# The transfers of the rows of maxima move from SyncE's queue to ScalarE's queue in a two-layer decoder kernel

## The chip, the core and the metric

The kernel runs on one core of a Trainium2 chip, as one launch. The time is that of the device in microseconds (us). A core has five engines that each work through their own instructions in order: TensorE (PE in the profile, its weight loads PEld), VectorE (DVE), ScalarE (ACT), GpSimd (POOL) and SyncE (SP), which here only issues transfers. Semaphores are all that ties them together.

## What is computed

Eight batches of x (256 tokens of 128 features) pass through six residual blocks, each on a layer norm of x:

```python
x = x + _L0_attn_ref(...)    # causal linear attention, 16 heads
x = x + _L0_xattn_ref(...)   # cross attention to 512 context tokens, 16 heads, masked softmax
x = x + _L0_ffn_ref(...)     # 8 experts, the best two by gate
x = x + _L1_attn_ref(...)    # causal attention in a window of 128, 16 heads
x = x + _L1_xattn_ref(...)   # cross attention, 8 heads, then layer norms and a ReLU FFN
x = x + _L1_ffn_ref(...)     # ternary weights, GELU FFN
```

In the softmax blocks the scores are q k / sqrt(head size), the largest score of each query is taken off, then follow exp, the sum over keys, and the product with the values.

## The kernel before

**Phases.** Each batch has four attention cores, `p` = 0 (linear), 1 (cross, 16 heads), 2 (window, 16 heads) and 3 (cross, 8 heads). Between two cores of a batch runs a *chain* ("to0", "to1", "to2", "to3", "end"): it normalizes the last core's outputs, projects them, adds them to x, runs the experts or the FFN, takes a layer norm and makes the next q, k and v. Three chains run side by side, in three lanes.

**Stacks.** q and k are each split into three BF16 parts, so that six products give an f32 score. The parts are written to a DRAM buffer of the lane (`bounce`, `spread` at L591 to L596) and read back as tall stacks: 48 rows per head hold the products, and further rows hold the negated maximum of each query (`QP`, `QW`, `KS`; `chain_steps` of SyncE, L605 to L638). There are three slots for stacks.

**Maxima.** For p = 1, 2 and 3 the *max stream* computes all scores once (PE L978 to L982), DVE reduces each to its maximum (L1467 to L1475), and per group of four heads GpSimd splits the negated maxima in three parts (L795 to L799). PE then turns them into rows (L970), and DVE copies these rows from PSUM to `mrow` (L1462), a ring of four buffers. This last step is a *turn*. There are 32 turns of p = 1, 32 of p = 2 and 16 of p = 3, 80 in all. After each turn the rows are sent by transfers into the stack of queries: two for p = 1 or 2 (L656), four for p = 3 (L652), 192 in all.

**Exponentials.** The *exp stream* computes the scores a second time (PE L1004 to L1013), now with the maxima in the stack taken off, into two PSUM banks; ACT takes exp (L1199, 512 units; for p = 0 DVE masks them at L1485), and PE multiplies by the values in quads of four units (L1039). ACT copies finished outputs out (L1206). Before the first unit of a group PE waits for that group's rows (`mrow_in`).

**The order of the work** is fixed when the program is built. `plan()` simulates the three lanes and the two streams with costs written by hand and gives each event a due time; `weave` merges, for each engine, the max events, the exp events and the steps of the three lanes by due time into one sequence. Every engine uses the same events and leaves out those it has no part in. A turn's due time is that of its last maximum plus `TURN_LATE` = 3.0. So an engine that waits at one event holds up all that stands behind it in its own sequence, of whatever lane or stream. At a turn SyncE waits for the copy on DVE (`max_used`), and then for the stack itself (`stack_in`), which has then been in use by the max stream.

ACT takes part in the exp stream, and in each chain: it makes the normalized rows (L1082), copies turned activations out of PSUM for the next matmul (L1075, L1136), keeps and casts q and k (L1107 to L1130), and computes the exponentials and GELUs of the FFNs. It has no part in the max stream: `program(nothing, exp_event, chain_steps, prelude())`.

Of the kernel before, what the change touches and what calls it, by code (L numbers as in the profile page):

```python
# [16 lines left out]
B, S, D, SK = 8, 256, 128, 512  # L17
# [3 lines left out]
PARTS = 3  # L21
# [23 lines left out]
MAX_ROWS = 4 * PARTS  # L45
HALF_ROWS = NPROD * 8
# [4 lines left out]
LANES, SLOTS, WIDES, OUTS, OB, QN, MROWS = 3, 3, 2, 3, 1, 3, 4  # L51
# [226 lines left out]
TURN_N = {(e.core.p, e.core.b, e.g): i for i, e in enumerate(TURNS)}  # L278
# [5 lines left out]
IN_SLOT, OUT_BEFORE = {}, {}  # L284
# [77 lines left out]
def weave(lanes):  # L362

    at = [next(lane, None) for lane in lanes]
    while any(t is not None for t in at):
        i = min((t, i) for i, t in enumerate(at) if t is not None)[1]
        at[i] = next(lanes[i], None)


def events_of(events, act):  # L370
    for e in events:
        yield e.at
        act(e)


def runs_of(lane, steps):
    for run in RUNS:
        if run.lane == lane:
            for at in steps(run):
                yield run.at(at)  # L380


def decoder(nc, x, ctxT, maskq, maskk, weights, columns, rows_in, experts_bias, out):
    with ExitStack() as ctx:
# [6 lines left out]
        def sem(name):  # L391
            return ctx.enter_context(nc.semaphore(name))

        def sems(n, *names):
            return [[sem(f"{name}_{i}") for i in range(n)] for name in names]

        def sbs(n, name, shape, dt=F32):
            return [sb(f"{name}{i}", shape, dt) for i in range(n)]
# [24 lines left out]
        QP = sbs(SLOTS, "QP", [P, 16, S], BF16)  # L423
        QW = sbs(WIDES, "QW", [P, 8, S], BF16)
# [7 lines left out]
        mrow = sbs(MROWS, "mrow", [MAX_ROWS, S], BF16)  # L432
# [52 lines left out]
        max_scores, max_used, nm_ready = sem("max_scores"), sem("max_used"), sem("nm_ready")  # L485
# [4 lines left out]
        stack_in, = sems(SLOTS, "stack_in")  # L490
        mrow_in, = sems(MROWS, "mrow_in")
# [9 lines left out]
        def w(name, lo=0, n=None):  # L501
            a, b = W_COLS[name]
            return W[:, a + lo:(a + lo + n) if n else b]
# [19 lines left out]
        def slot_emptied(eng, run):  # L523

            old, _, _ = IN_SLOT[run.new.p, run.b]
            if old:
                eng.wait_ge(av_done, UNITS_TO[old.p, old.b])
# [20 lines left out]
        def program(max_event, exp_event, chain_steps, *more):  # L548
            weave([events_of(MAX_EVENTS, max_event), events_of(EXP_EVENTS, exp_event)]
                  + [runs_of(lane, chain_steps) for lane in range(LANES)] + list(more))  # L550
# [7 lines left out]
        def _(sp):  # L558
# [24 lines left out]
            def ctx_loads(lane):  # L583
                for run in (r for r in CTX_RUNS if r.lane == lane):
                    last = [r for r in CTX_RUNS if r.lane == run.lane and r.start < run.start]
                    yield max(run.start - 8 * STRETCH, last[-1].end if last else 0)
                    if last:
                        sp.wait_ge(lane_free[run.lane], N_RUNS(last[-1]) + 1)
                    sp.dma_start(cT[run.lane][:], ctxT[run.b:run.b + 1].rearrange("o p t -> p (o t)")).then_inc(ctx_in[run.lane], 16)
# [47 lines left out]
                if p == 3:  # L637
                    sp.dma_start(QW[core.wide][HALF_ROWS:64], back[NPROD * 16:NPROD * 16 + 16, :, 0:S]).then_inc(stack_in[slot], 16)  # L638

            def max_event(e):  # L640
                if e.kind != "turn":
                    return
                core, g = e.core, e.g
                ring = TURN_N[core.p, core.b, g] % MROWS
                row_ = mrow[ring]
                sp.wait_ge(max_used, e.n + 3)

                sp.wait_ge(stack_in[core.slot], IN_SLOT[core.p, core.b][2])
                if core.p == 3:
                    for j in range(4):  # L650
                        at = HALF_ROWS + 2 * PARTS * (j % 2)
                        sp.dma_start(QW[core.wide][at:at + PARTS, 4 * g + j, :], row_[PARTS * j:PARTS * (j + 1), :]).then_inc(mrow_in[ring], 16)  # L652
                else:
                    for r in range(2):
                        at = 64 * r + HALF_ROWS
                        sp.dma_start(QP[core.slot][at:at + MAX_ROWS, 4 * g + r:4 * g + 4:2, :],  # L656
                                     row_[:].unsqueeze(1).to_broadcast([MAX_ROWS, 2, S])).then_inc(mrow_in[ring], 16)

            program(max_event, nothing, chain_steps, *(ctx_loads(lane) for lane in range(LANES)))
            sp.wait_ge(x_out, B * 16)  # L660

        @block.gpsimd
# [404 lines left out]
        def _(act):  # L1067
# [123 lines left out]
            def exp_event(e):  # L1191
# [8 lines left out]
                elif e.kind == "keep":  # L1200
# [4 lines left out]
                        act.wait_ge(filled[last.lane], fill(last, "outputs"))  # L1205
                    nc.scalar.copy(OT[core.out][:, 2 * e.g:2 * e.g + 2, :].rearrange("p g q -> p (g q)"), ob[:, e.n % OB, :]).then_inc(out_kept, 1)  # L1206

            def prelude():
                yield 18.0
                act.wait_ge(w_in[3], 16)  # L1210
                for i in range(2):
                    ins = nc.scalar.activation(wtmp[:, i, :], w(("up", "down")[i]), ACT.Abs, accum_out=absum[:, i:i + 1])
                ins.then_inc(act_const, 1)
                yield 24
                act.wait_ge(ternary_ready, 1)

            program(nothing, exp_event, chain_steps, prelude())

        @block.vector
        def _(dve):  # L1220
# [336 lines left out]
```

## Times and profile before

| | us |
|---|---|
| median of three runs | 1142.5 |
| lowest, highest | 1141.14, 1148.11 |
| the profiled execution: its own time | 1149.97 |
| its span | 1148.3 |
| busy: PE, PEld | 867.2, 484.1 |
| busy: DVE, ACT, POOL | 664.9, 496.5, 327.2 |
| granted clock of TensorE, mean | 0.898 |

The span is that of the recorded instructions, and what lies around it is 1.67 us. Busy time does not count SyncE's issues, nor the time in which ACT or any other engine waits for a semaphore. The profile comes from one execution that is 7.5 us longer than the median.

### The profile page before, as it was taken

Reading aid. Unit: us, or ns where it says so; the run is one execution under the profiler, and the core shown is the slowest. Engines: PE = TensorE matmul, PEld = TensorE weight load, DVE = VectorE, ACT = ScalarE, POOL = GpSimd, SP = SyncE. Lnnn points to the kernel's source line nnn. Section 1 sums busy time; section 2 is a strip of 40 time slices with the busy share of each in tenths; the row PEclk is TensorE's granted clock in tenths of the full one; section 3 lists DMA queues with packets and bytes.
Section 4 is the critical chain, followed back from the end, with each engine's and each line's share of the span. In section 5 each row is a group of like instructions: output and inputs, shape, how many; then the busy total and the mean of one; then the engine's idle time right before and its main releaser. Section 6 shows DMA issues by size and latency. Waiting matters only on the chain.

```text
span 1148.3 us, 19620 instructions
## 1 busy us (share of the span) xinstructions
PE 867.2 (76%) x6459; PEld 484.1 (42%) x6522; DVE 664.9 (58%) x2234; ACT 496.5 (43%) x1019; POOL 327.2 (28%) x872
## 2 busy tenths in 40 slices
PE   0576757989887887878787677887988777875666
PEld 0354534334333443434443455653533435652345
DVE  5656546767677664766667574376566484334431
ACT  1332314544545443545464333654545334652432
POOL 7414323111212221323212235322222124341032
PEclk9888879999999988989889888999999698896877
DMA  5467764033021214541233434652120602224100
GB/s 177 113 98 160 166 147 90 19 49 53 20 48 30 38 32 85 110 97 52 56 56 68 71 80 104 143 86 39 34 53 16 103 2 52 66 64 75 16 1 10
DMA packets 124965, 79.85 MB, mean 70 GB/s; under 512 B 8312, under 2 KB 122176, under 8 KB 124736
## 3 DMA queue, kind: packets, MB, share of 16 engines
q1 hardware_dynamic: 124864, 78.59, 33.4%
q8 instruction: 52, 0.85, 0.3%
q14 instruction: 49, 0.40, 0.1%
HBM read 43.99 MB, written 32.90 MB: 67 GB/s over the span
## 4 chain that ended last, share of the span: by engine, by line
PE 46%; DVE 18%; issue 10%; DMA 9%; POOL 6%; ACT 6%; SPq 4%; another core or an unknown queue 0%; DVEq 0%; POOLq 0%; ACTq 0%
PE ob L1039 8%; PE mb L982 5%; DMA KS<-bounce 4%; PE side L858 3%; DMA QW<-bounce 3%; PE eb L1009 3%; DVE junk L1467 3%; PE eb L1010 2%; PE side L913 2%; DVE mx L1475 2%; PE side L905 2%; PE side L896 2%; DVE An L1407 2%; PE side L925 1%; PE eb L1004 1%
## 5 line engine op out<-in xcount | busy, mean ns | idle before, releaser
L1199 ACT ACTIVATE probs<-eb 128x512 f32<-128x512 f32 (+1 forms) x512 | 287.6, 570 | 379.3 <-PE eb L1010 162.1
L1467 DVE CUSTOM_DVE_ANT_0 junk<-mb,maskq_add 128x512 bf16<-128x512 f32 x256 | 172.2, 690 | 118.3 <-PE mb L982 90.0
L795 POOL TENSOR_SCALAR nm<-mx 128x8 bf16<-128x8 f32 x80 | 20.3, 254 | 455.5 <-DVE mx L1467 206.5
L1039 PE MATMUL ob<-probs,V 128*32 128x256 f32 (+1 forms) x2048 | 142.1, 399 | 1.9 <-ACT probs L1199 0.7
L1475 DVE TENSOR_REDUCE mx<-mb 128x1 f32<-128x512 f32 x128 | 84.9, 687 | 68.3 <-PE mb L982 66.5
L1009 PE MATMUL eb<-maskk_add,identb 128*128 128x512 bf16 x256 | 100.1, 391 | 6.5 <-DMA QP<-mrow 2.7
L982 PE MATMUL mb<-KS,QP 128*128 128x512 bf16 x230 | 89.3, 395 | 13.5 <-DVE mx L1467 12.8
L1010 PE MATMUL eb<-QP,KS 128*128 128x512 bf16 x233 | 91.2, 391 | 0.0
L1039 PEld LDWEIGHTS ob<-probs,V 128*32 128x32 f32 x2048 | 56.2, 115 | 79.1 <-issue 49.0
L1470 DVE CUSTOM_DVE_ANT_0 junk<-mb,winq_add 128x128 bf16<-128x128 f32 x128 | 37.1, 290 | 77.1 <-PE mb L979 75.3
L982 PE MATMUL mb<-KS,QW 112*128 112x512 bf16 x128 | 53.1, 433 | 32.7 <-DMA QW<-bounce 19.2
L818 PE MATMUL side<-ident,hn 128*128 128x128 f32 x80 | 19.6, 332 | 66.3 <-ACT hn L1082 66.2
L1206 ACT COPY OT<-ob 128x512 f32<-128x512 f32 x56 | 32.6, 582 | 68.9 <-PE ob L1033 48.0
L1485 DVE TENSOR_TENSOR probs<-eb,tri 128x512 f32<-128x512 f32 x64 | 42.1, 685 | 32.0 <-PE eb L999 30.6
L715 POOL TENSOR_TENSOR xs<-xs,scratch 128x256 f32<-128x256 f32 (+1 forms) x32 | 30.4, 951 | 104.0 <-ACT scratch L1130 63.2
L858 PEld LDWEIGHTS side<-ident,OT 128*128 128x128 f32 x448 | 55.7, 198 | 8.0 <-issue 6.7
L1013 PE MATMUL eb<-QW,KS 112*128 112x256 bf16 x256 | 51.5, 298 | 9.5 <-DMA QW<-mrow 3.1
L858 PE MATMUL side<-ident,OT 128*128 128x36 f32 (+1 forms) x448 | 55.6, 280 | 3.8 <-issue 3.7
L703 POOL TENSOR_SCALAR rstd<-mv 128x2 f32<-128x2 f32 x64 | 19.6, 307 | 134.3 <-DVE mv L1263 131.5
L982 PEld LDWEIGHTS mb<-KS,QP 128*128 128x128 bf16 x256 | 25.7, 101 | 69.9 <-DVE mx L1467 40.9
L1082 ACT ACTIVATE hn<-X,nshift,rstd 128x128 f32<-128x128 f32 x80 | 35.1, 488 | 45.8 <-POOL nshift L710 45.8
L1471 DVE CUSTOM_DVE_ANT_0 junk<-mb,winq_add 128x256 bf16<-128x256 f32 x128 | 53.7, 419 | 0.2 <-issue 0.2
(188 smaller groups left out, 1728.3 us busy)
## 6 DMA issues: line engine op xcount, KB each, us to landing
QP<-bounce SPq DMA_DIRECT2D x48, 256.0 KB, 5.6
KS<-bounce SPq DMA_DIRECT2D x32, 384.0 KB, 7.5
bounce<-scratch SPq DMA_DIRECT2D x48, 192.0 KB, 2.3
bounce<-scratch SPq DMA_DIRECT2D x64, 128.0 KB, 2.0
KS<-bounce SPq DMA_DIRECT2D x32, 192.0 KB, 6.0
bounce<-scratch SPq DMA_DIRECT2D x16, 384.0 KB, 2.6
cT<-ctxT_dram SPq DMA_DIRECT2D x16, 256.0 KB, 2.9
bounce<-scratch SPq DMA_DIRECT2D x16, 256.0 KB, 3.1
```

Of the source, the lines that this page charges most:

```text
L858: ins = nc.tensor.matmul(bank[:, lo:lo + 4 * n].rearrange("p (h e) -> p h e", e=n), OT[o][:, g, t * P:(t + 1) * P], chosen, start=True, st ...
L982: ins = nc.tensor.matmul(bank, q_of(core, h)[:, 0, t * P:(t + 1) * P], k_of(core, h, 0, SK), start=True, stop=True)
L1009: nc.tensor.matmul(part, identb[:], maskk_add[:, kt:kt + 1, :].to_broadcast([P, 2, S]), start=True, stop=False, skip_group_check=True)
L1010: ins = nc.tensor.matmul(part, k_of(core, h, kt * P, P), q_of(core, h, 2), start=False, stop=True, skip_group_check=True)
L1013: ins = nc.tensor.matmul(bank[:, j * S:(j + 1) * S], k_of(core, h + j, kt * P, P), q_of(core, h + j)[:, 0, :], start=True, stop=True)
L1039: ins = nc.tensor.matmul(bank[32 * j:32 * j + 32, S - n:S], v_of(core, kt, 4 * g + j), pr[:, (j % 2) * n:(j % 2 + 1) * n], start=(kt == 0) ...
L1199: nc.scalar.activation(probs[:, u % PROBS, 0:n], eb[:, u % 2, 0:n], ACT.Exp, scale=SCALE[core.p]).then_inc(probs_by[1], 1)
L1467: ins = V_.tensor_tensor_reduce(junk[:, e.n % 2, :], bank, maskq_add[:, t, :], 1.0, NEG_EXP, ALU.add, ALU.max, mx[slot][:, t, h:h + 1])
L1470: V_.tensor_tensor_reduce(junk[:, e.n % 2, 0:P], bank[:, 0:P], winq_add[:, 0, :], 1.0, NEG_EXP, ALU.add, ALU.max, mx[slot][:, 0, h:h + 1])
L1471: ins = V_.tensor_tensor_reduce(junk[:, e.n % 2, P:3 * P], bank[:, P:3 * P], winq_add[:, 1:3, :].rearrange("p a k -> p (a k)"), 1.0, NEG_E ...
L1475: ins = V_.tensor_reduce(mx[slot][:, t, h:h + 1], bank, AX.X, ALU.max)
L1485: V_.tensor_tensor(probs[:, u % PROBS, :].rearrange("p (j q) -> p j q", j=4), eb[:, u % 2, :].rearrange("p (j q) -> p j q", j=4), tri[:].u ...
```

## The change

The function `max_event` of SyncE is moved to ScalarE, word for word but for the engine: the same waits, the same 192 transfers, the same semaphores. It takes its place in ScalarE's sequence by the due time of the turn. SyncE now has no part in the max stream.

```diff
@@ SyncE
-            def max_event(e):
-                ...
-                sp.wait_ge(max_used, e.n + 3)
-
-                sp.wait_ge(stack_in[core.slot], IN_SLOT[core.p, core.b][2])
-                ...
-            program(max_event, nothing, chain_steps, *(ctx_loads(lane) for lane in range(LANES)))
+            program(nothing, nothing, chain_steps, *(ctx_loads(lane) for lane in range(LANES)))
@@ ScalarE
+            def max_event(e):
+                if e.kind != "turn":
+                    return
+                core, g = e.core, e.g
+                ring = TURN_N[core.p, core.b, g] % MROWS
+                row_ = mrow[ring]
+                act.wait_ge(max_used, e.n + 3)
+
+                act.wait_ge(stack_in[core.slot], IN_SLOT[core.p, core.b][2])
+                if core.p == 3:
+                    for j in range(4):
+                        at = HALF_ROWS + 2 * PARTS * (j % 2)
+                        act.dma_start(QW[core.wide][at:at + PARTS, 4 * g + j, :], row_[PARTS * j:PARTS * (j + 1), :]).then_inc(mrow_in[ring], 16)
+                else:
+                    for r in range(2):
+                        at = 64 * r + HALF_ROWS
+                        act.dma_start(QP[core.slot][at:at + MAX_ROWS, 4 * g + r:4 * g + 4:2, :],
+                                     row_[:].unsqueeze(1).to_broadcast([MAX_ROWS, 2, S])).then_inc(mrow_in[ring], 16)
...
-            program(nothing, exp_event, chain_steps, prelude())
+            program(max_event, exp_event, chain_steps, prelude())
```

## Rows read from the trace of the kernel before

**Rows 1.** The page, busy time by engine, and the chain that ended last by engine

```profile
PE 867.2 (76%) x6459; PEld 484.1 (42%) x6522; DVE 664.9 (58%) x2234; ACT 496.5 (43%) x1019; POOL 327.2 (28%) x872
...
PE 46%; DVE 18%; issue 10%; DMA 9%; POOL 6%; ACT 6%; SPq 4%; another core or an unknown queue 0%; DVEq 0%; POOLq 0%; ACTq 0%
```

**Rows 2.** Waits: waiter <- releaser: us in total, times, longest

```profile
ACT probs L1199 <- PE eb L1010: 162.1, 135, 7.8
...
PEld eb L1013 <- ACT probs L1199: 10.1, 21, 1.1
```

**Rows 3.** The tile mrow: ns min/median/max, first and last start in us

```profile
L656 SPq DMA_DIRECT2D QP<-mrow x128: 778/790/1417, 173.0 to 1014.3; - x128
L1462 DVE COPY mrow<-mb x80: 268/274/281, 172.7 to 1085.6; 12x256 bf16<-12x256 bf16 x80
L652 SPq DMA_DIRECT2D QW<-mrow x64: 639/641/778, 562.0 to 1088.0; - x64
```

**Rows 4.** Waits of the DMA queue of SyncE

```profile
SPq L656 <- DVE mrow L1462: 270.6, 53, 11.4
SPq L652 <- DVE mrow L1462: 103.1, 14, 11.9
```

**Rows 5.** The chain in order of time: start, us, what; first and last pieces

```profile
189.36 0.16 SPq L656
...
1087.27 0.64 SPq L652
1087.95 1.67 DMA QW<-mrow
```

**Rows 6.** The page, DMA issues: KB each, us from issue to landing

```profile
bounce<-scratch SPq DMA_DIRECT2D x16, 256.0 KB, 3.1
```

**Rows 7.** Timeline of SyncE, 555 to 565: start, us, instruction

```profile
555.22 2.02 SPq L596 DMA_DIRECT2D bounce<-scratch  x4
561.96 2.81 SPq L652 DMA_DIRECT2D QW<-mrow  x4
564.89 0.58 SPq L635 DMA_DIRECT2D QP<-bounce  x1
```

**Rows 8.** Timeline of PE, instructions that a transfer released, [idle before <-releaser]

```profile
191.60 0.39 PE L1009 MATMUL eb<-maskk_add,identb 128*128 128x512 bf16 x1 [2.67 <-DMA QP<-mrow]
...
441.04 0.22 PE L978 MATMUL mb<-KS,QP 128*128 128x128 bf16 x1 [2.96 <-DMA KS<-bounce]
454.55 1.19 PE L925 MATMUL side<-cT,W 128*128 128x512 f32 x1 [2.96 <-DMA cT<-ctxT_dram]
508.50 1.19 PE L925 MATMUL side<-cT,W 128*128 128x512 f32 x1 [3.97 <-DMA cT<-ctxT_dram]
573.20 0.27 PE L978 MATMUL mb<-KS,QP 128*128 128x128 bf16 x1 [6.80 <-DMA KS<-bounce]
...
667.65 0.27 PE L978 MATMUL mb<-KS,QP 128*128 128x128 bf16 x1 [4.38 <-DMA KS<-bounce]
...
1066.77 0.59 PE L982 MATMUL mb<-KS,QW 112*128 112x512 bf16 x1 [5.09 <-DMA QW<-bounce]
```

**Rows 9.** Timeline around the turn copied by 225.25: DVE, ACT, PE

```profile
224.97 0.28 DVE L1462 COPY mrow<-mb 12x256 bf16<-12x256 bf16 x1 [0.72 <-PE mb L970]
...
224.92 0.58 ACT L1206 COPY OT<-ob 128x512 f32<-128x512 f32 x1 [0.46 <-PE ob L1039]
...
226.38 0.38 PE L1009 MATMUL eb<-maskk_add,identb 128*128 128x512 bf16 x1
```

**Rows 10.** Timeline behind the first turn: ACT, PE

```profile
172.28 0.88 ACT L1082 ACTIVATE hn<-X,nshift,rstd 128x128 f32<-128x128 f32 x2
...
173.21 0.44 PE L818 MATMUL side<-ident,hn 128*128 128x128 f32 x2
```

**Rows 11.** Timeline behind the last turn: ACT, PE

```profile
1085.91 1.08 ACT L1199 ACTIVATE probs<-eb 128x512 f32<-128x512 f32 x2 [0.57 <-PE eb L1013]
...
1087.47 0.38 PE L1013 MATMUL eb<-QW,KS 112*128 112x256 bf16 x2
```

More of the change, by code:

```diff
@@ L638, in chain_steps @@
                     sp.dma_start(QW[core.wide][HALF_ROWS:64], back[NPROD * 16:NPROD * 16 + 16, :, 0:S]).then_inc(stack_in[slot], 16)
-            def max_event(e):
[L641 to L645, printed above, removed]
-                sp.wait_ge(max_used, e.n + 3)
-                sp.wait_ge(stack_in[core.slot], IN_SLOT[core.p, core.b][2])
[L649 to L657, printed above, removed]
-            program(max_event, nothing, chain_steps, *(ctx_loads(lane) for lane in range(LANES)))
+            program(nothing, nothing, chain_steps, *(ctx_loads(lane) for lane in range(LANES)))
             sp.wait_ge(x_out, B * 16)
```

## The prediction, as it was put on record

> **What bounds the kernel now.** I read the page first, then the waits, the answers for `mrow`, the chain that ended last, and timelines around single turns. No engine is full: PE is busy 867.2 of 1148.3 us, DVE 664.9, ACT 496.5, and the chain that ended last goes from engine to engine, 46% of it on PE, 18% on DVE, 10% issue, 6% on ACT, 4% in SyncE's queue [rows 1]. So the time is set by hand-overs between sequences whose order is fixed, PE being most often the one that others wait for. ACT follows PE: it waits 162.1 us for one line of scores alone, PE's weight loads wait for its exponentials 10.1 us [rows 2]. ACT's 652 us without work look like room. They come in pieces of half a microsecond to two, and whether a piece lies where the new work falls is the question here.
>
> A turn's transfers are issued at 0.790 us each for p = 1, 2 (128 of them, up to 1.417) and 0.641 us for p = 3 (64) [rows 3]. A turn thus holds SyncE's queue for about 1.65 us with 2 issues, 2.8 with 4. SyncE also waits ahead of them for the copy on DVE: 270.6 us in 53 turns and 103.1 us in 14 [rows 4]. The issue starts 0.03 us behind the copy in 76 of the 80 turns, so the rows of maxima themselves are hardly ever late through SyncE; what stands behind them there is.
>
> **What SyncE gets back.** The turn's waits and issues leave its queue. Worked example: four spreads are issued from 555.22 on and end at 557.24; a spread of this kind lands 3.1 us after issue [rows 6], so the read-back of the stacks could start at about 560.2. SyncE stood at the turn until the copy of 561.93, issued four transfers, and began the read-back at 564.89, some 4.7 us late [rows 7]. PE waited 6.80 us for that stack, to 573.20 [rows 8]. Seven such places have a PE wait that a transfer ended, of 2.67, 2.96, 2.96, 3.97, 6.80, 4.38 and 5.09 us [rows 8]. The lateness in SyncE there, worked out the same way, is 5.0 (here the rows of maxima stood behind spreads that waited for ACT), 2.8, 3.0, 1.6, 4.7, 11.3 and 5.5. The smaller of the two at each place sums to 24 us, the most that can come back. The least: the chain runs over the issues of turns themselves, 22 pieces from 189.36 to 1087.27 [rows 5] with 14.6 us in sum; without the last turn's 1.9, which only change their engine, 12.6. The PE waits for a stack from 910.9 and 1041.0 have no turn ahead of them in SyncE and stay. Between 12.6 and 24 I take **18 us**, the middle, since after a stack comes early something else ends the wait.
>
> **What ACT takes on.** ACT meets the turn at its due place, waits for the copy, and issues 192 transfers. No row shows an issue on ACT. Bounds: nothing, if its sequencer could issue under the calculation before it, and 1.417 us each, the longest of SyncE's. I take SyncE's own medians, the same instruction with the same operands. Most turns leave no calculation to hide under, because the copy ends later than ACT's last work before it, by 0.76 us in the median turn. Three examples, each delay being copy end + issues − old start of ACT's next instruction:
> - first turn, copied at 173.0: 1.8 us of issues end at 174.8, the normalization L1082 that started at 172.28 is 2.55 us late. PE took it at 173.21 and passes on 2.5 [rows 3, 10].
> - a turn copied at 225.25: issues to 226.9, L1206 started at 224.92, so 1.95 late; the four exponentials behind it run back to back, and PE's scores at 226.38, two units further, are 1.7 late [rows 9].
> - last turn, copied at 1085.86: issues to 1088.6, ACT's exponentials of 1085.91 are 2.7 late, PE's scores of 1087.47 are 2.2 late [rows 11].
>
> Taken so over all 80 turns, the first and the last of them given, ACT is late by 142 us in sum: issues of 152 us, 24 us of waiting for copies beyond the gap that was there, less the gaps. I followed each delay along ACT until a later gap swallowed it, and took off the time between the end of each result and the start of its first user. In 26 turns nothing is passed on. The rest pass 72 us to PE or DVE: 24 in p = 1, 25 in p = 2, 23 in the 16 turns of p = 3 with their four issues. Where PE is late, all is late only if PE is on the chain at that time, which it is for 46%, with the issue time 56% [rows 1]: 0.56 × 72 = **40 us**. Ends: nothing, and the whole 72, or more if an issue costs more on ACT.
>
> **Other edits.** The stack's wait that moves along (`stack_in`) is long passed when the turn comes, since PE's max stream waited for the same landing. The transfers land after 1.67 us on the chain [rows 5] and use the same engines; nothing changes there.
>
> On the issue's weight: the rows show two issues of 0.79 us ahead of a landing of about 2. By the Trainium skill (DMA: Bandwidth & Descriptors, section Issuing engines are not separate DMA queues) issuing from several engines only saves the sequencer's time to start a DMA, which is "usually small relative to the DMA itself". By that rule neither side of this sum would weigh much, which is the second rival. The row disagrees on "small": with these tiny transfers the issues take as long as the landing.
>
> **Sum.** 1149.97 + 40 − 18 = 1172 us in the profiled execution's own terms. That execution lay 7.5 us above the median of its runs, so against the median 1142.5 + 22 = **1164 us**.
>
> **Rivals.**
> 1. *ACT's idle time hides the issues and only SyncE's gain stays* (faster). Place: the waits of rows 8; price 24 us, and 1142.5 − 24 = 1118; half of it, 1130, if ACT keeps a little. For: PE hardly ever waits for exponentials [rows 2], 26 turns pass nothing on, issues can overlap a running calculation. Against: the copy ends behind ACT's last work, and the chains' small results (L1082, L1136) are used at once. It decides if less than 15% of the 142 us gets through.
> 2. *The two cancel*, within 11 us: 1142.5 + 20 − 20 = 1142. It needs the 72 us to count for a quarter only, PE's own 281 us without work taking up the rest.
> 3. *All that is passed on reaches the end*: 1142.5 + 72 − 12 = 1202. PE waits in order, so a delay of its scores holds back the max stream and all three lanes, then the next copy, at which ACT waits again. For: p = 3's turns pass on 1.5 us on average. Against: where DVE sets the pace, PE has room.
>
> **Chances.** Forecast (slower by 11 to 45 us) 0.46; cancel 0.26; hidden and faster by more than 11 us 0.16; more than 45 us slower 0.12. One per cent, 11.4 us, is about what can be told from no change here. So faster 0.16, same 0.26, slower 0.58. The range goes from 1131, the first rival at half its price, to 1202, the third at its full one.
>
> **What the profile after would show.** SyncE's queue without L652 and L656, the read-back behind 560 starting some 4 us earlier against its spreads, and shorter PE waits for `KS<-bounce` and `QW<-bounce`. On ACT, 192 issues of 0.6 to 0.8 us, starting right behind each copy; ACT's busy time unchanged, but PE's and DVE's waits for ACT clearly up (L1082, L1199, L1136), by tens of us. The chain should have ACT's queue in it in SyncE's place, at several per cent. I am wrong if issues on ACT take a few tenths, or if those waits grow while the end doesn't move.

## The result and the profile after

The changed kernel takes 1222.68 us (median of four runs, 1218.52 to 1224.88) against 1143.98 before. The ratio is 1.0681, with a 95% interval of 1.0635 to 1.0727, so the change costs 78 us. The direction was as forecast, the size was not: the range ended at 1202.

The profiled execution has a span of 1216.8 us. First the page of the changed kernel, its busy time, the chain by engine, and what ScalarE's and SyncE's queues carry (packets, MB, share of 16 engines):

```profile
PE 893.5 (73%) x6459; PEld 493.2 (41%) x6522; DVE 667.6 (55%) x2234; ACT 492.6 (40%) x1019; POOL 327.5 (27%) x872
...
q1 hardware_dynamic: 119872, 76.92, 31.0%
q10 hardware_dynamic: 4992, 1.68, 0.7%
...
PE 22%; DVE 6%; issue 5%; ACT 5%; ACTq 3%; DMA 1%; POOL 1%; SPq 0%; DVEq 0%; POOLq 0%
```

Against [rows 1] DVE, ScalarE and GpSimd are busy within 4 us of before. PE is busy 26.3 us longer, with the same 6459 recorded matmuls and a lower granted clock:

```profile
core 0: 1148.3 us, clock 0.898
core 0: 1216.8 us, clock 0.882
```

The trace has two levels of that clock, full (2.4 GHz) and half (1.2 GHz). Worked out from the means, PE was granted the lower one for some 234 us before and 287 us now. So of the 68.5 us by which the span grows, PE waits in 42.2 and takes longer over the same work in 26.3.

ScalarE's queue now stands in the chain and SyncE's does not. The shares sum to 43% only, since the chain could be followed back only to 670.6 us, so they are no ledger.

The tile `mrow` in the changed kernel (ns min/median/max, first and last start), which answers to [rows 3]:

```profile
L1205 ACTq DMA_DIRECT2D QP<-mrow x128: 789/790/1442, 171.9 to 1079.4; - x128
L1462 DVE COPY mrow<-mb x80: 269/274/281, 171.6 to 1153.3; 12x256 bf16<-12x256 bf16 x80
L1201 ACTq DMA_DIRECT2D QW<-mrow x64: 667/676/724, 585.9 to 1155.7; - x64
```

An issue costs on ScalarE what it cost on SyncE, 0.790 us, and 0.676 in place of 0.641 for p = 3. The first copy is 1.1 us earlier than before, the last 67.7 later; the whole loss of the span (68.5 us) is made between the first turn and the last. It comes all along the span: 10.4 us by the ninth turn, 20 by the 33rd, 40 by the 49th, 61 by the 69th.

PE's waits in the changed kernel (us in total, times, longest), for ScalarE and for transfers:

```profile
PE side L799 <- ACT hn L1063: 81.7, 29, 20.4
PE side L850 <- ACT hT L1117: 16.8, 7, 5.3
PE eb L994 <- ACT probs L1180: 15.1, 13, 3.5
PE eb L990 <- ACT probs L1180: 12.9, 17, 2.2
...
PE side L906 <- DMA cT<-ctxT_dram: 17.9, 4, 6.6
PE mb L963 <- DMA QW<-bounce: 11.5, 2, 7.2
```

and the same lines in the kernel before (its L818, L869, L1013, L1009, L925, L982, and one that is gone):

```profile
PE side L818 <- ACT hn L1082: 66.2, 28, 20.4
PE side L869 <- ACT hT L1136: 5.2, 1, 5.2
PE eb L1013 <- ACT probs L1199: 3.0, 7, 0.9
PE eb L1009 <- ACT probs L1199: 1.0, 3, 0.5
...
PE side L925 <- DMA cT<-ctxT_dram: 21.2, 5, 6.4
PE mb L982 <- DMA QW<-bounce: 19.2, 4, 7.3
PE mb L978 <- DMA KS<-bounce: 14.1, 3, 6.8
```

Both sides of the sum are there. On these lines PE waits 25 us less for transfers (of [rows 8] the three waits for `KS` are gone) and 51 us more for ScalarE, and every instruction behind a waiting one on PE waits too. Summed over all lines of the same view, PE's waits for ScalarE grow from 100 to 174 us, those for transfers fall from 61 to 32, those for DVE from 77 to 71. With 3 us from the rest that makes the 42 us. The 100 us before were mostly the wait for `hn`, which [rows 2] does not show; it is ScalarE's result for a chain, not an exponential.

What one turn looks like now: the turn of [rows 9], ScalarE, DVE and PE in the changed kernel:

```profile
231.03 1.28 ACT L1180 ACTIVATE probs<-eb 128x512 f32<-128x512 f32 x2 [1.01 <-PE eb L991]
233.12 1.64 ACTq L1205 DMA_DIRECT2D QP<-mrow  x2
234.86 0.59 ACT L1187 COPY OT<-ob 128x512 f32<-128x512 f32 x1 [2.55 <-DVE mx L1467]
235.34 1.09 ACT L1180 ACTIVATE probs<-eb 128x512 f32<-128x512 f32 x2
...
232.81 0.28 DVE L1462 COPY mrow<-mb 12x256 bf16<-12x256 bf16 x1 [0.72 <-PE mb L951]
...
236.00 0.39 PE L990 MATMUL eb<-maskk_add,identb 128*128 128x512 bf16 x1 [1.61 <-ACT probs L1180]
236.23 0.38 PE L991 MATMUL eb<-QP,KS 128*128 128x512 bf16 x1
236.44 0.38 PE L963 MATMUL mb<-KS,QP 128*128 128x512 bf16 x1
```

ScalarE's exponentials end at 232.31. It waits 0.78 us for the copy, which ends at 233.09, and issues until 234.76: it stands 2.45 us, of which 0.46 was its gap before. PE then waits 1.61 us at 236.00 for an exponential, and the max stream's matmul L963 stands behind that wait. So the next maxima are late, and with them the next copy, at which ScalarE waits again. Over the 80 turns ScalarE waits 93 us in 65 turns (before, the copy ended behind its last work by 99 us in 66), issues for 150 us, and stands 240 us between the end of its last work and the end of the last issue. In 71 of 80 turns its next instruction starts within 0.2 us of the issue's end: nothing is left of the gap. PE notices it: in 47 of the 80 turns it waits for one of ScalarE's next two instructions, 65 us in sum, and before it did so in 6 turns, for 4 us.

### The profile page after: what moved, and what is told of

Read it like the earlier page. It is cut to its first block and busy times, and to the rows that moved or that the text cites. A ratio compares the mean times of both kernels' runs of the same rounds, so it can differ in the third digit from the quotient of the medians.

```text
span 1216.8 us, 19620 instructions
## 1 busy us (share of the span) xinstructions
PE 893.5 (73%) x6459; PEld 493.2 (41%) x6522; DVE 667.6 (55%) x2234; ACT 492.6 (40%) x1019; POOL 327.5 (27%) x872
## 5 line engine op out<-in xcount | busy, mean ns | idle before, releaser
L1180 ACT ACTIVATE probs<-eb 128x512 f32<-128x512 f32 (+1 forms) x512 | 284.1, 570 | 406.0 <-PE eb L991 121.4
L1020 PE MATMUL ob<-probs,V 128*32 128x256 f32 (+1 forms) x2048 | 150.6, 418 | 3.9 <-ACT probs L1180 2.6
L963 PE MATMUL mb<-KS,QP 128*128 128x512 bf16 x230 | 89.7, 396 | 12.5 <-DVE mx L1467 11.6
L799 PE MATMUL side<-ident,hn 128*128 128x128 f32 x80 | 22.1, 369 | 81.8 <-ACT hn L1063 81.7
L994 PE MATMUL eb<-QW,KS 112*128 112x256 bf16 x256 | 55.8, 316 | 25.9 <-ACT probs L1180 15.1
L963 PE MATMUL mb<-KS,QW 112*128 112x512 bf16 x128 | 55.8, 456 | 23.1 <-DMA QW<-bounce 11.5
L1063 ACT ACTIVATE hn<-X,nshift,rstd 128x128 f32<-128x128 f32 x80 | 34.9, 487 | 55.5 <-POOL nshift L691 42.2
L963 PEld LDWEIGHTS mb<-KS,QP 128*128 128x128 bf16 x256 | 26.0, 102 | 65.3 <-DVE mx L1467 34.7
```

Of the source, the lines that this page charges most:

```text
L963: ins = nc.tensor.matmul(bank, q_of(core, h)[:, 0, t * P:(t + 1) * P], k_of(core, h, 0, SK), start=True, stop=True)
L994: ins = nc.tensor.matmul(bank[:, j * S:(j + 1) * S], k_of(core, h + j, kt * P, P), q_of(core, h + j)[:, 0, :], start=True, stop=True)
L1020: ins = nc.tensor.matmul(bank[32 * j:32 * j + 32, S - n:S], v_of(core, kt, 4 * g + j), pr[:, (j % 2) * n:(j % 2 + 1) * n], start=(kt == 0) ...
L1063: ins = nc.scalar.activation(dst[:, t, :], src[:, t, :], ACT.Identity, bias=nshift[l][:, t:t + 1], scale=rstd[l][:, t:t + 1])
L1180: nc.scalar.activation(probs[:, u % PROBS, 0:n], eb[:, u % 2, 0:n], ACT.Exp, scale=SCALE[core.p]).then_inc(probs_by[1], 1)
```

## The experiments

Ratios are against the kernel before on the same chip; us in brackets are the ratio times 1144.

**Wait alone.** ScalarE waits for the copy, SyncE issues as before.

```diff
+            def max_event(e):
+                if e.kind == "turn":
+                    act.wait_ge(max_used, e.n + 3)
-            program(nothing, exp_event, chain_steps, prelude())
+            program(max_event, exp_event, chain_steps, prelude())
```

> The kernel before, with one thing added: at each of the 80 turns ScalarE waits for the copy to mrow, and issues nothing; SyncE keeps all 192 transfers. Theory A (the issues on ScalarE are the cost, the wait is mostly covered by the gap that was there: 24 us beyond the gaps, about half of it on the chain): 1144 + 5 to 15, so 1149 to 1159. Theory B (the wait ties the exp stream to the max stream, each delay of one now delays the other, and that is why more than the 72 us came): 1144 + 35 or more.

1.0034, 1.0008 to 1.0060 (+4). Tying ScalarE to the max stream costs next to nothing, a little less than theory A had for it. Theory B falls.

**Issues alone.** As many spare transfers on ScalarE, without the wait; the real ones on SyncE.

```diff
+        spare = [nc.dram_tensor(f"spare{i}", (P, 4, S), BF16, kind="Internal").ap() for i in range(MROWS)]
+        spare_row = winq_add[0:MAX_ROWS].rearrange("p a q -> p (a q)")[:, 0:S]
...
+                if n >= MROWS:
+                    act.wait_ge(spare_in[ring], MROW_TO[n - MROWS])
...
+                else:
+                    for r in range(2):
+                        at = 64 * r + HALF_ROWS
+                        act.dma_start(spare[ring][at:at + MAX_ROWS, r:4:2, :],
+                                     spare_row.unsqueeze(1).to_broadcast([MAX_ROWS, 2, S])).then_inc(spare_in[ring], 16)
```

> The kernel before, and at each turn ScalarE issues as many transfers of the same shapes without waiting for the copy, from a constant tile into spare DRAM that nobody reads (it only waits that the spare transfer of four turns ago has landed); SyncE keeps the real ones. Theory A: the 150 us of issues carry the cost, all but a small part of the +92 us that would stand against SyncE's gain of 24: 1144 + 60 to 90. Theory B: the issues without the wait can be taken up by ScalarE's idle time: 1144 + 30 or less.

1.0031, 1.0006 to 1.0056 (+4). Theory A falls as well, in the form in which it was put: the issues alone, 122 us of them, are nearly free (theory B had this run at 30 or less, but it had fallen with the run before). The same turn, ScalarE with spare issues and no wait, shows why:

```profile
220.80 1.28 ACT L1203 ACTIVATE probs<-eb 128x512 f32<-128x512 f32 x2 [1.01 <-PE eb L1014]
221.49 1.56 ACTq L1236 DMA_DIRECT2D spare<-winq_add  x2
223.15 0.58 ACT L1210 COPY OT<-ob 128x512 f32<-128x512 f32 x1 [1.07 <-DMA spare<-winq_add]
```

The issue starts at 221.49 while the exponentials run until 222.08. In the median turn it starts 0.59 us before ScalarE's last work ends, and ScalarE stands 67 us in sum, not 240. With the wait ahead of it (rows above) the issue starts 0.81 us behind that end.

**No transfers.** The 192 transfers and SyncE's waits are gone, PE waits for the copy, and DVE no longer waits for a buffer of `mrow` to have been sent before it fills it again. This and the later runs without real transfers leave out that the maxima get into the scores.

```diff
-            program(max_event, nothing, chain_steps, *(ctx_loads(lane) for lane in range(LANES)))
+            program(nothing, nothing, chain_steps, *(ctx_loads(lane) for lane in range(LANES)))
-                    pe.wait_ge(mrow_in[n % MROWS], MROW_TO[n])
+                    pe.wait_ge(max_used, TURNS[n].n + 3)
```

> The kernel before without the 192 transfers: SyncE neither waits nor issues at a turn, and PE waits for the copy to mrow where it waited for the rows in the stack. It leaves out that the maxima get into the scores. It shows what SyncE gets back, with some 3 us more at each of the few places where the rows themselves were late. Both theories as on record: 12 to 24 us faster, so 1120 to 1132. A third theory, that the gain in SyncE's queue is worth nothing: 1144 less at most 5.

0.9732, 0.9695 to 0.9769 (−31), more than expected.

**GpSimd in ScalarE's place.** The same function on GpSimd.

> The 192 transfers with their waits on GpSimd in place of ScalarE, at the same due place; SyncE is relieved as in the change. GpSimd is busy 28% and does little at this place but chain steps of the layer norms. Theory A (what hurts is the blocked queue of an engine that both streams need): near or below 1144, 1125 to 1150. Theory B the same. If instead any engine that takes the waits and issues costs tens of us, 1170 or more.

1.0101, 1.0048 to 1.0154 (+12). The time, 1154 to 1156, is a little above theory A's 1125 to 1150. GpSimd waits 121.6 us in 67 turns for the copy and issues at 0.601 and 0.512 us. That costs 12 us more than SyncE's relief gives, where the same on ScalarE costs 78 more. A blocked queue is much cheaper there than on ScalarE.

**Wait and issues.** The two harmless edits together.

```diff
+                act.wait_ge(max_used, e.n + 3)
                 if n >= MROWS:
                     act.wait_ge(spare_in[ring], MROW_TO[n - MROWS])
```

> As the kernel with spare transfers on ScalarE, and now ScalarE first waits at each turn for the copy to mrow. SyncE keeps the real transfers. Theory C, formed from the runs with the wait alone (+3) and the issues alone (+3): either fits in the gap that ScalarE has at a turn and the issues alone run under the exponential before them, but wait and issue one behind the other do not fit; the changed kernel stands 110 us above the kernel without transfers, and here the narrow spare transfers take 0.29 us in place of 0.68, some 25 us less blocking: 1144 + 70 to 95. Rival D (the costs add up, and the change is slow through something else, such as rows that arrive later or two queues disturbing each other): 1144 + 4 to 15.

1.0623, 1.0583 to 1.0663 (+71). Two edits of 4 us each make 71 together. The same turn:

```profile
230.98 1.28 ACT L1203 ACTIVATE probs<-eb 128x512 f32<-128x512 f32 x2 [1.01 <-PE eb L1014]
233.07 1.56 ACTq L1237 DMA_DIRECT2D spare<-winq_add  x2
234.73 0.59 ACT L1210 COPY OT<-ob 128x512 f32<-128x512 f32 x1 [2.48 <-DVE mx L1492]
```

This is the changed kernel's picture, without any of its rows depending on ScalarE. Rival D (late rows, two queues) can explain at most what is left.

**Later in ScalarE's sequence**, by 1.5 and by 3.0 us of the plan's time; real transfers, SyncE relieved.

```diff
+            def late_turns():
+                for e in TURNS:
+                    yield e.at + 1.5
+                    max_event(e)
-            program(max_event, exp_event, chain_steps, prelude())
+            program(nothing, exp_event, chain_steps, prelude(), late_turns())
```

> The changed kernel with each turn's place in ScalarE's sequence 1.5 us later in the plan's time; all else the same. Theory C: ScalarE does its next piece of work first, the copy is there when it comes, and the issue starts under that work; the blocking falls from 240 us to near 100, and most of the 78 us goes, with SyncE's relief (31) on the other side: 1115 to 1150. Rival D: the same 192 issues on ScalarE, the rows later still: 1222 or more.

> The same with 3.0 us. Theory C: as little blocking as with 1.5, but the rows come later than the exp stream wants them (it is planned 4.5 behind the turn, and issue and landing take 3.5 of it), so 0 to 40 us slower than with 1.5. Rival D: slower than the changed kernel, above 1222.

1.0071, 1.0037 to 1.0105 (+8), and 1.0245, 1.0208 to 1.0282 (+28). Nothing is changed but the place, and 70 of the 78 us go. The first is 2 to 4 us above what theory C had for it, 1115 to 1150. The turn with 1.5 us: ScalarE, then DVE's copy:

```profile
226.41 0.58 ACT L1187 COPY OT<-ob 128x512 f32<-128x512 f32 x1 [0.46 <-PE ob L1020]
227.20 0.60 ACT L1180 ACTIVATE probs<-eb 128x512 f32<-128x512 f32 x1 [0.20 <-PE eb L991]
227.26 1.61 ACTq L1205 DMA_DIRECT2D QP<-mrow  x2
228.97 1.08 ACT L1180 ACTIVATE probs<-eb 128x512 f32<-128x512 f32 x2 [1.17 <-DVE mx L1472]
...
226.46 0.28 DVE L1467 COPY mrow<-mb 12x256 bf16<-12x256 bf16 x1 [0.72 <-PE mb L951]
```

The copy is there before ScalarE comes, and the issue starts 0.06 us behind the start of an exponential. ScalarE waits for a copy in 11 turns, not 65, and stands 135 us. With 3.0 us it stands 129, hardly less, and the issue of the rows starts 2.1 us behind the copy in the median turn, not 0.6. PE's waits for rows with 3.0 us (its weight loads and its matmuls show the same waits):

```profile
PEld eb L994 <- DMA QW<-mrow: 20.4, 5, 7.2
PE eb L994 <- DMA QW<-mrow: 19.1, 5, 6.9
```

**Only the 64 turns of p = 1, 2 on ScalarE**, at the due place and, in a later run, 1.0 us later. SyncE keeps p = 3.

```diff
@@ SyncE, then ScalarE
-                if e.kind != "turn":
+                if e.kind != "turn" or e.core.p != 3:
...
+                if e.kind != "turn" or e.core.p == 3:
```

> The changed kernel, but the 16 turns of p = 3 with their four transfers stay on SyncE; the 64 turns with two transfers are on ScalarE. Theory C: the 64 turns hold 159 of the 240 us of blocking, and SyncE gets back a part: 1144 + 40 to 60. If the cost were in the four-issue turns: 1144 + 0 to 20. If the costs went with the number of turns alone: 1144 + 62.

> The 64 turns of p = 1 and 2 on ScalarE, 1.0 us later in the plan's time, and the 16 of p = 3 left on SyncE, whose four issues no single exponential hides. Theory C: little blocking on ScalarE, part of SyncE's relief, no late rows for p = 3: 1125 to 1148. If it stands above 1155, the issues cost even where they start under running work.

1.0487, 1.0421 to 1.0553 (+56), and 1.0052, 1.0018 to 1.0085 (+6). The turns with two issues are enough for most of the loss, and the place decides here too. The second is no better than all turns 1.5 later, and lies just above the 1125 to 1148 expected.

**Relieved and blocked.** Wait and spare transfers on ScalarE, no real transfers.

> The kernel with wait and spare transfers on ScalarE, and now without the 192 real transfers on SyncE (PE waits for the copy instead of the rows, so the maxima do not get into the scores). Against that kernel (+72) it shows what SyncE's relief is worth while ScalarE is blocked. If the whole 31 us of the run without transfers come back: 1145 + 41, so 1180 to 1190. If less, since ScalarE's blocking then sets the pace and the stacks are no longer what PE waits for (as on record, 12.6 or more; the changed kernel at +78 with some 20 us more of blocking than +72 points to it): 1195 to 1208.

1.0306, 1.0248 to 1.0364 (+35). Against +71 the whole gain comes back (36 us with an interval of some 8 either way, against 31 alone). A blocked ScalarE does not devalue SyncE's relief.

**Half the issues** behind the wait.

```diff
-                    for j in range(4):
+                    for j in range(2):
-                    for r in range(2):
+                    for r in range(1):
```

> The kernel with wait and spare transfers on ScalarE (+72), with half the spare transfers per turn: one for p = 1 and 2, two for p = 3. Blocking some 60 us less. If each microsecond of issue behind the wait goes through alike: halfway between the wait alone (+3) and +72, so 1145 + 30 to 45. If only what exceeds the gap of a turn counts: 1145 + 5 to 20.

1.0175, 1.0123 to 1.0227 (+20), at the upper end of the second expectation and well below halfway (+38).

**GpSimd later**, by 1.0 us, and then with p = 3 at its due place (`yield e.at + (0.0 if e.core.p == 3 else 1.0)`).

```diff
+            def late_turns():
+                for e in TURNS:
+                    yield e.at + 1.0
+                    turn_event(e)
-            program(max_event, nothing, chain_steps, values())
+            program(max_event, nothing, chain_steps, values(), late_turns())
```

> The real transfers on GpSimd with its place 1.0 us later in the plan's time than in the run at +1.0% there. If what it lost there is the wait for the copy (121.6 us in 67 turns) in front of its chain steps: 1125 to 1145, which would beat the kernel before. If the issues or their latency are the loss: 1150 or more.

> The real transfers on GpSimd, the turns of p = 1 and 2 1.0 us later in the plan's time, those of p = 3 at their due place, because PE waited 13 us for QW<-mrow where all were later. If that was the loss: 4 to 10 us faster than the 1143 of that run, 1133 to 1139, and so faster than the kernel before by about 1%. Otherwise 1140 to 1150.

0.9969, 0.9939 to 1.0000 (−3), and 1.0029, 1.0004 to 1.0054 (+3). The first is the best version found, but its interval reaches 1.0000, so it can't be told from no change. The second refutes the guess that p = 3's later rows were its loss.

**SyncE blocked by spare transfers** (PE waits for the copy), and **ScalarE blocked by the same**. Each turn of p = 3 has three wide spares and a narrow one, 2.7 us, so the blocking is of the real length.

```diff
+        def spares(eng, core, ring):
+            for r in range(3 if core.p == 3 else 2):
+                at = 64 * (r % 2) + HALF_ROWS
+                eng.dma_start(spare[ring][at + 12 * (r // 2):at + 12 * (r // 2) + MAX_ROWS, r % 2:4:2, :],
+                              spare_row.unsqueeze(1).to_broadcast([MAX_ROWS, 2, S])).then_inc(spare_in[ring], 16)
+            if core.p == 3:
+                eng.dma_start(spare[ring][0:PARTS, 0, :], spare_row[0:PARTS, :]).then_inc(spare_in[ring], 16)
```

> The kernel without the real transfers (the maxima do not get into the scores, PE waits for the copy), and SyncE again waits at each turn and issues two spare transfers for p = 1 and 2, four for p = 3 (three of the wide form and one narrow, some 2.6 us). It stands between the kernel before and the one without transfers (-31): what it is above the latter is the worth of SyncE's relief, what it is below the former is the worth of rows that need no issue and no landing. If the relief is what was recorded, 12.6 to 24: 1145 - 18 to -7, so 1127 to 1138. If nearly all of the 31 is relief: 1142 or more. If the landing is all: 1115 to 1120.

> The same spare transfers with the wait on ScalarE, SyncE free, no real transfers. Against the run with relief and blocking (+36, p = 3's four issues 0.29 us each there) it has full-length issues at the 16 turns of p = 3, as the changed kernel has. The changed kernel differs then only by rows that have to land. If p = 3's longer issues, some 20 us more blocking, make most of the 41 us between them: 1200 to 1215. If the landing makes it: 1185 to 1195.

0.9934, 0.9906 to 0.9961 (−8), and 1.0543, 1.0493 to 1.0594 (+62). With the run without transfers they divide the change:

| step | from, to | us |
|---|---|---|
| SyncE's relief | 0.9934, 0.9732 | −23 |
| ScalarE waits and issues | 0.9732, 1.0543 | +93 |
| real rows in place of spares: before | 0.9934, 1.0000 | +8 |
| real rows in place of spares: after | 1.0543, 1.0681 | +16 |

So −23 + 93 + 16 − 8 = +78. The intervals of the ratios make each step uncertain by 3 to 8 us. The narrow spares of 0.29 us gave +35 where these gave +62, so some 27 us go with the issue length in 16 turns of p = 3 (16 us between the profiled executions, at 0.903 and 0.900).

As far as the profiles show, the +16 is not PE waiting for rows. The profiled executions of four runs, all with the same number of recorded matmuls (span less busy time is what PE waits; PE's waits for ScalarE and for `mrow` rows are sums of its lines):

| run | span | PE busy | PE waits | of it for ScalarE | for rows | clock |
|---|---|---|---|---|---|---|
| before | 1148.3 | 867.2 | 281.1 | 100 | 6 | 0.898 |
| SyncE blocked by spares | 1140.8 | 862.4 | 278.4 | 104 | 0 | 0.904 |
| ScalarE blocked by spares | 1194.6 | 872.8 | 321.8 | 178 | 0 | 0.900 |
| the change | 1216.8 | 893.5 | 323.3 | 174 | 3 | 0.882 |

```profile
core 0: 1194.6 us, clock 0.900
PE 872.8 (73%) x6459; PEld 484.1 (41%) x6522; DVE 665.4 (56%) x2234; ACT 492.6 (41%) x1019; POOL 329.1 (28%) x872
```

Between the last two, PE waits 1.5 us more and is busy 20.7 us more. The four executions of ScalarE blocked by spares took 1196, 1204, 1214 and 1210 us at granted clocks of 0.900, 0.887, 0.879 and 0.879, the change 1219, 1225, 1222 and 1223 at 0.882, 0.872, 0.883 and 0.876. So a part of the +16 goes with the clock; at like clocks, 0.876 to 0.883, some 10 us are left, which nothing accounts for.

## Why the prediction went wrong

**SyncE's gain** was right. 18 us were taken between 12.6 and 24; it is 23, uncertain by some 5. It lies nearer the upper end, at each place the smaller of SyncE's lateness and PE's wait, but 18 is not excluded.

**Issue length** on ScalarE was right: 0.790 and 0.676 us against 0.790 and 0.641 taken, with the wait in front of it where it was expected, 93 us against 99.

**The step that failed** is the last of ScalarE's side, "0.56 × 72 = 40 us", and with it the claim that "where PE is late, all is late only if PE is on the chain". The term measured 93 us. Three things bear on it:
- The 72 us passed on are about what came. PE's waits for ScalarE grow by 74 us in the change, and by 72 from the run without transfers to ScalarE blocked by spares (105 to 178). How near that is may be luck: the 72 counted DVE too, and the gaps were taken from the trace before, as if each turn found them new.
- The factor 0.56 was wrong. The share of PE in the chain was taken for the chance that a delay matters. From the run without transfers to ScalarE blocked by spares, the profiled span grows by 84 us, against 72 us more of waits for ScalarE: nothing like half of them was lost on the way. PE's instruction that waits for an exponential has the max stream behind it, and the copy that ScalarE waits for comes from the max stream. That this loop through ScalarE, PE, DVE and back is why PE's delays count in full is argued from the rows around 236; the runs show only its sum.
- The clock had no term in the sum. All four executions of the change were granted 0.872 to 0.883 and those of wait and issues 0.879 to 0.884, while the 70 executions of the kernel before that were timed beside the experiments lie between 0.893 and 0.912. In the profiles that is 26 of the 68.5 us. Why the clock falls in the kernels with the most blocking stays open.

How steep the cost is can be read from four runs. The overhang is what reaches beyond ScalarE's gaps, an estimate from the turns of the trace before, good to a few us. PE's waits for ScalarE are the sums over its lines, less those of the run that each is compared with.

| run | overhang | PE's waits for ScalarE | cost |
|---|---|---|---|
| wait alone | 25 | +7 | 4 |
| half the issues | 68 | +24 | 20 |
| all spares, with the wait | 119 | +57 | 71 |
| the change (waits and cost from ScalarE blocked by spares) | 142 | +72 | 93 |

The first 25 us of overhang are almost free, the next 43 cost 0.4 each, the rest about 1.0 each. Part of that last price is the clock, since the two dear kernels are also those at the lowest clocks. A fixed share, as I used, is the wrong shape.

**Rivals.** "The issues hide in ScalarE's idle time" is true of the issues, and true of the wait, each alone (+4 us each). It fails for the two in a row: the wait takes the gap and moves the issue out from under the running exponentials. The third rival, all that is passed on reaches the end (1202), named the right mechanism as far as the runs show one, and had 0.12. It was still 20 us short, though it took off only 12 us for SyncE, and not through its 72: the clock was missing in it too. The second, that both cancel, needed a quarter of the 72 to count, and all of it did.

On the Trainium skill's sentence that the issuing time is "usually small relative to the DMA itself" (DMA: Bandwidth & Descriptors, section Issuing engines are not separate DMA queues): here 150 us of issues behind a wait cost up to 93 us, while 122 us of them under running work cost 4. The size of an issue says little without its place.

**Open.** Why the granted clock is lower in the most blocked kernels, and what makes up the rest of the +16. That it is 8 us more than the +8 before is inside the intervals of the ratios. Why GpSimd at the due place costs 12 us and 1 us later nothing was not followed up either; its four executions at the due place were granted 0.892 to 0.898, the ten with 1 us more 0.900 to 0.909.

## What to carry to other kernels

A transfer moved to an engine that calculates costs little if its wait is already met when the engine gets there, since the issue then runs under the calculation before it; if the wait is for something just being made, wait and issue add up in a row, and their sum beyond the engine's gap is the price. Shift such an event in the engine's sequence until the wait is met, and no further than its user allows. Where two streams share in-order engines, count a repeated delay in full once it exceeds the slack, and don't scale it by the share of the chain. And split a loss into PE's waits and PE's busy time: where the second grows with the same matmuls, look at the granted clock.

## What the runs showed of the hardware

ScalarE starts the issue of a transfer while its own calculation runs: at 221.49 under exponentials that ended at 222.08, at 227.26 under one of 227.20 to 227.80. A sequence of two issues takes 1.6 us there all the same. The next calculation starts 0.10 us behind the second.

An issue of 3 partitions by 256 BF16 takes 0.676 us on ScalarE from `mrow` into SBUF. From a constant tile into DRAM the same size takes 0.293 where four of them follow each other, and 0.456 behind three wide ones. On GpSimd the real issues took 0.60 and 0.51 us, less than on SyncE (0.790 and 0.641), but the first starts 0.29 us behind the copy in the median turn, on SyncE and ScalarE 0.03.

The same 6459 recorded matmuls kept PE busy 867.2 us at a mean granted clock of 0.898, 872.8 at 0.900 and 893.5 at 0.882.
